# Dense rows as three exact bf16 parts times fp16 count panels, 16 panel groups, 336 edge tiles counted

## The reference, cut to what matters

```python
def _L0_gnn_ref(x, edge_index, weight, bias):
    summed = jax.ops.segment_sum(x[src], dst, num_segments=n)
    deg = jax.ops.segment_sum(jnp.ones_like(src, dtype=x.dtype), dst, num_segments=n)
    agg = summed / jnp.maximum(deg, 1.0)[:, None]
    out = jnp.concatenate([x, agg], axis=-1) @ weight
    out = out / jnp.linalg.norm(out, axis=-1, keepdims=True)
    return out + bias

def _forward(feats, ...):                       # layer 1
    h = feats * jax.lax.rsqrt(deg_out)[:, None]
    m = jax.ops.segment_sum(h[src], dst, num_segments=n) * jax.lax.rsqrt(deg_in)[:, None]
    x = m @ W_gc + b_gc + (feats @ W_res + b_res)
    y = x + _moe_ff(x, Wg, bg, w1, b1, w2, b2)
    ...                                         # batch norm over the nodes

x = _layernorm(x + _L0_gnn_ref(x, edge_index, ...), axis=-1)
x = _layernorm(x + _L1_gnn_ref(x, ..., src, dst), axis=-1)
```

## Time and profile before

| | |
|---|---|
| median of 3 runs | 2753.98 us (2734.45 to 2765.64) |
| the profiled execution | 2723.63 us, its span 2721.7 us |
| granted clock of TensorE, mean | 0.889 |
| PE busy | 2033.4 us, 75% |
| DVE, ACT, POOL busy | 1284.5, 605.1, 1364.6 us |
| moved by DMA | 304.32 MB |
| layer 0's steps | about 57 to 946 us of the span |
| layer 1's steps | about 1053 to 1888 us |

### The profile page before, as it was taken

One profiled execution on the slowest core, in us unless ns is written; L12 is line 12 of the kernel. 1 busy time (PEld: TensorE's weight loads), 2 busy tenths in 40 slices (PEclk: granted clock), 3 DMA queues, 4 the chain that ended last, 5 costly groups with the idle time before them and its releaser, 6 DMA issues.

```text
span 2721.7 us, 49652 instructions
## 1 busy us (share of the span) xinstructions
PE 2033.4 (75%) x15088; PEld 1633.2 (60%) x15088; DVE 1284.5 (47%) x3827; ACT 605.1 (22%) x1544; POOL 1364.6 (50%) x1353
## 2 busy tenths in 40 slices
PE   2788888888787573788888888885653788888847
PEld 1566666767666451567666666763542677777735
DVE  6655666766665484433433333322434232232275
ACT  0211112212121052211111211111323222222227
POOL 4655566556556674555555455564446334443410
PEclk9788899999998795899999999997776899999968
DMA  4323333333323504322232233234100776547772
GB/s 150 97 88 91 89 89 104 94 94 108 92 86 88 173 6 143 88 86 82 82 87 83 72 88 88 78 89 162 43 31 18 218 230 206 158 132 220 216 226 98
DMA packets 217122, 304.32 MB, mean 112 GB/s; under 512 B 46418, under 2 KB 164233, under 8 KB 216956
## 3 DMA queue, kind: packets, MB, share of 16 engines
q0 software_dynamic: 58576, 146.85, 18.8%
q1 hardware_dynamic: 103388, 101.82, 11.7%
q10 hardware_dynamic: 54992, 53.49, 6.2%
HBM read 289.58 MB, written 57.83 MB: 128 GB/s over the span
## 4 chain that ended last, share of the span: by engine, by line
PE 43%; issue 14%; DVE 14%; another core or an unknown queue 13%; SPq 6%; DMA 3%; DVEq 2%; ACT 2%; POOL 1%; POOLq 0%; ACTq 0%
PE bank L1095 16%; PE bank L1117 3%; PE bank L1051 3%; PE bank L1113 3%; PE bank L1131 3%; PE bank L1066 3%; PE bank L1294 3%; DVE oh_lo L1481 3%; PE bank L1303 2%; DVE oh_hi L1481 2%; PE bank L1192 2%; DVE Y L1898 1%; DVE codes L1503 1%; DMA acc<-x_scratch,acc 1%
## 5 line engine op out<-in xcount | busy, mean ns | idle before, releaser
L707 POOL DMA_INDIRECT gath<-in_x_dram,idx_t x480 | 532.7, 1110 | 393.8 <-PE bank L1051 242.7
L1095 PE MATMUL bank<-Y,X 128*128 128x128 f32 x5096 | 682.3, 289 | 28.2 <-issue 26.8
L1095 PEld LDWEIGHTS bank<-Y,X 128*128 128x128 f32 x5096 | 661.5, 204 | 58.6 <-issue 41.4
L707 POOL DMA_INDIRECT gath<-h_scratch,idx_t x480 | 467.6, 974 | 389.8 <-PE bank L1051 225.1
L837 ACT ACTIVATE Y<-bank 128x400 f32<-128x400 f32 (+1 forms) x416 | 184.1, 494 | 1066.0 <-remote 615.1
L1503 DVE TENSOR_SCALAR codes<-iota_code,code_t 128x784 bf16<-128x784 f16 x456 | 175.4, 426 | 274.2 <-remote 211.0
L1481 DVE TENSOR_TENSOR oh_lo<-iota_lo,lohi_t 128x512 bf16<-128x512 bf16 x392 | 269.2, 687 | 40.3 <-remote 32.0
L1515 DVE TENSOR_TENSOR acc<-acc,bank 128x256 f32 x240 | 101.2, 422 | 372.5 <-issue 356.1
L1113 PE MATMUL bank<-codes,oh_lo 128*128 128x400 bf16 x456 | 164.7, 362 | 121.1 <-DVE oh_hi L1481 54.8
L1117 PE MATMUL bank<-codes,oh_lo 128*128 128x384 bf16 x456 | 163.6, 359 | 79.0 <-issue 53.0
L802 POOL DMA_INDIRECT y_scratch<-acc x96 | 97.6, 1017 | 221.1 <-DVE acc L1875 206.2
(11 more groups left out here) (244 smaller groups left out, 2568.4 us busy)
## 6 DMA issues: line engine op xcount, KB each, us to landing
acc<-in_L_gnn_w_dram SPq DMA_DIRECT2D x101, 512.0 KB
acc<-in_L_gnn_w_dram ACTq DMA_DIRECT2D x96, 512.0 KB
y_scratch<-bias_s ACTq DMA_DIRECT2D x49, 256.0 KB
y_scratch<-bias_s SPq DMA_DIRECT2D x98, 128.0 KB
Y<-y_scratch SPq DMA_DIRECT2D x14, 896.0 KB
acc<-in_L_gnn_b_dram ACTq DMA_DIRECT2D x96, 128.0 KB
gath<-in_x_dram,idx_t POOLq DMA_INDIRECT x480
gath<-h_scratch,idx_t POOLq DMA_INDIRECT x480
```

Source lines behind the costliest of these rows:

```text
L707: pool.indirect_dma_start(out=gath[:, half, k, :], out_offset=None, in_=table, in_offset=bass.IndirectOffsetOnAxis(ap=idx_t[:, TD + t:TD + ...
L1095: last = pe.matmul(DB[w % 2][:, c * P:(c + 1) * P], X[:, h, c * P:(c + 1) * P], panel[:, w % 2, h, :], start=(h == 0), stop=(h == NT - 1))
```

## The change

Each fp32 number of X is split into three bf16 parts whose sum is the number: its upper 16 bits (`x_top`, read in place as every second bf16), the rest rounded to bf16 (`x_mid`, in Y's memory), and what is left (`x_low`, written over the lower 16 bits in X). The panels are kept in fp16, in half of Y, and a slice becomes three bf16 by fp16 products into the same bank. PE makes the rests (`rests`: identity in fp32 minus the top; `lows`: minus the middle) in the two banks of `dense`, which are free before the first group, and ACT copies them out; 25 cuts of two row tiles, six ahead of step 0 and four in each of the first five steps. As X no longer holds x after this, `turn_x` puts the three parts together by three products where the tile is cut already, and X is loaded again behind the last dense product, interleaved with Y. The plan grows from 304 to 336 counted tiles, with 8 more panels of two tiles and 16 of one; a layer has 56 steps, windows of three steps after a lead of two, 16 groups, and up to three panel additions a step. ACT clears `acc` in place of POOL.

```diff
-PANEL_TILES = ((8, 9), (4, 21), (2, 74))
-GROUP_PANELS = ((1, 1, 6),) * 9 + ((0, 2, 6), (0, 4, 4)) * 2
-WINDOW = 4
-ADDS = 2
+PANEL_TILES = ((8, 9), (4, 21), (2, 82), (1, 16))
+GROUP_PANELS = ((1, 1, 6, 0),) * 9 + ((0, 2, 6, 0), (0, 4, 4, 0)) * 2 + ((0, 0, 8, 0), (0, 0, 0, 8), (0, 0, 0, 8))
+WINDOW = 3
+LEAD = 2
+ADDS = 3
...
+    cut = [(i, 2) for i in range(NT - 2, 0, -2)] + [(0, 1)]
+    EARLY, PER_STEP = 6, 4
...
+    turned_whole = [cut_of[i] >= EARLY + PER_STEP * i + PER_STEP // 2 for i in range(NT)]
...
-            units_at[WINDOW * w + u * WINDOW // len(units)].append((w,) + unit)
+            units_at[WINDOW * w + LEAD + u * WINDOW // len(units)].append((w,) + unit)
         for k in range(WINDOW):
-            slices_at[WINDOW * (w + 1) + k] = (w, SLICES * k // WINDOW, SLICES * (k + 1) // WINDOW)
+            slices_at[WINDOW * (w + 1) + LEAD + k] = (w, SLICES * k // WINDOW, SLICES * (k + 1) // WINDOW)
...
-        panel = yflat.rearrange("p (b h n) -> p b h n", b=2, h=NT)
+        panel = yflat[:, 0:NT * P].bitcast(F16).rearrange("p (b h n) -> p b h n", b=2, h=NT)
+        x_mid = yflat[:, NT * P:2 * NT * P].bitcast(BF16).rearrange("p (t d) -> p t d", t=NT)
+        x_halves = X[:, :, :].rearrange("p t d -> p (t d)").bitcast(BF16).rearrange("p (t d k) -> p t d k", t=NT, k=2)
+        x_low, x_top = x_halves[:, :, :, 0], x_halves[:, :, :, 1]
+        x_parts = (x_top, x_mid, x_low)
...
                 for k in range(SEVEN):                      # SP, load_back
                     sp.dma_start(Y[:, SEVEN * k:SEVEN * (k + 1), :], ...).then_inc(y_back, 16)
+                    if L == 1:
+                        sp.dma_start(X[:, SEVEN * k:SEVEN * (k + 1), :], tile_rows(h_d, P * SEVEN * k, SEVEN, P)
+                                     ).then_inc(x_again, 16)
+                    ...                                     # the same from x in layer 0
...
-                    if L == 0 and t == 2 * GROUP:           # POOL
-                        pool.memset(acc[:, :, :], 0.0).then_inc(acc_step, 1)
...
+            pool.wait_ge(x_again, 16 * (SEVEN + 1))
             in_pairs(pool, NT, stage)
-            for b in range(2):
-                pool.wait_ge(sums_staged[b], (NT + 1 - b) // 2)
-            pool.memset(acc[:, :, :], 0.0).then_inc(acc_step, 1)
...
+            def keep_mids(L, first):                        # ACT; keep_lows alike: low_left, x_low, low_made
+                for k in range(first, min(first + 2, len(cut))):
+                    i, n = cut[k]
+                    act.wait_ge(rest_made, len(cut) * L + k + 1)
+                    act.activation(x_mid[:, i:i + n, :].rearrange("p t d -> p (t d)"), DB[k % 2][:, 0:n * D], ACT.Copy
+                                   ).then_inc(mid_made, 1)
...
             for st in range(ST):
+                first_cut = EARLY + PER_STEP * st
+                keep_mids(1, first_cut)
+                keep_lows(1, first_cut)
                 keep_panels(1, st)
                 if st < NT:
                     turned_x(1, st)
+                keep_mids(1, first_cut + 2)
                 keep_part(1, st)
+                keep_lows(1, first_cut + 2)
...
+            def rests(L, first):                            # PE
+                ...
+                    if k > 1:
+                        pe.wait_ge(low_made, q - 1)
+                    o = DB[k % 2][:, 0:n * D]
+                    pe.matmul(o, ident[:, :], X[:, i:i + n, :].rearrange("p t d -> p (t d)"), start=True, stop=False)
+                    pe.matmul(o, minus_i[:, :], x_top[:, i:i + n, :].rearrange("p t d -> p (t d)"),
+                              start=False, stop=True).then_inc(rest_made, 1)
+
+            def lows(L, first):
+                ...
+                    pe.wait_ge(mid_made, len(cut) * L + k + 1)
+                    pe.matmul(DB[k % 2][:, 0:n * D], minus_i[:, :], x_mid[:, i:i + n, :].rearrange("p t d -> p (t d)"),
+                              start=False, stop=True, skip_group_check=True).then_inc(low_left, 1)
...
-                    last = pe.matmul(DB[w % 2][:, c * P:(c + 1) * P], X[:, h, c * P:(c + 1) * P], panel[:, w % 2, h, :],
-                                     start=(h == 0), stop=(h == NT - 1))
+                    for k, part in enumerate(x_parts):
+                        last = pe.matmul(DB[w % 2][:, c * P:(c + 1) * P], part[:, h, c * P:(c + 1) * P], panel[:, w % 2, h, :],
+                                         start=(h == 0 and k == 0), stop=(h == NT - 1 and k == len(x_parts) - 1))
...
+                rests(L, first_cut)                         # in step, and again behind turn_x
                 dense(L, st, lo, lo + (hi - lo) // chunks)
                 if st > 0:
                     shift(L, st - 1)
+                lows(L, first_cut)                          # and again behind prep
```

More of the change, by code:

```diff
@@ L119, in gnn_kernel @@
     BY_DVE = 4
+    cut = [(i, 2) for i in range(NT - 2, 0, -2)] + [(0, 1)]
+    EARLY, PER_STEP = 6, 4
+    assert len(cut) <= EARLY + PER_STEP * (WINDOW + LEAD)
+    cut_of = {j: k for k, (i, n) in enumerate(cut) for j in range(i, i + n)}
+    turned_whole = [cut_of[i] >= EARLY + PER_STEP * i + PER_STEP // 2 for i in range(NT)]
     SLICES = DC * NT
@@ L847, in keep_part, with clear_sums @@
                                ACT.Copy).then_inc(part_ready, 1)
+            def clear_sums(cols):
+                n = cols.stop - cols.start if isinstance(cols, slice) else 2 * P
+                return act.activation(acc[:, :, cols], small[:, 12:13].unsqueeze(2).to_broadcast([P, DC, n]), ACT.Copy)
             act.wait_ge(fill_set, 2)
+            clear_sums(slice(0, ACCW)).then_inc(acc_step, 1)
+            for k in range(0, EARLY, 2):
+                keep_mids(0, k)
+                keep_lows(0, k)
             for st in range(ST):
+                first_cut = EARLY + PER_STEP * st
                 if st < NT:
@@ L1036, in _ @@
             pe.wait_ge(tabs_made, 4)
[L1037 removed]
+            pe.matmul(banks[1][0:1, 0:1], small[:, 9:10], ones_c[:, 0:1], start=True, stop=True
                       ).then_inc(flag_summed, 1)
+            pe.wait_ge(tabs_done, 2 * CH)
+            pe.wait_ge(const_set, 8)
+            groups_in = set()
+            def rests(L, first):
+                for k in range(first, min(first + 2, len(cut))):
+                    i, n = cut[k]
+                    q = len(cut) * L + k
+                    if L == 0:
+                        for g in sorted({i // SEVEN, (i + n - 1) // SEVEN} - groups_in):
+                            pe.wait_ge(x_in[g], 32 if g == SEVEN - 1 else 16)
+                            groups_in.add(g)
+                    if k > 1:
[5 more added lines that the diff above has]
+            def lows(L, first):
+                for k in range(first, min(first + 2, len(cut))):
+                    i, n = cut[k]
+                    pe.wait_ge(mid_made, len(cut) * L + k + 1)
+                    pe.matmul(DB[k % 2][:, 0:n * D], minus_i[:, :], x_mid[:, i:i + n, :].rearrange("p t d -> p (t d)"),
+                              start=False, stop=True, skip_group_check=True).then_inc(low_left, 1)
+            for k in range(0, min(EARLY, 8), 2):
+                rests(0, k)
+                lows(0, k)
             pe.wait_ge(win_set, 1)
[L1040 removed]
             pe.wait_ge(weights_in, 3 * 16)
+            for k in range(8, EARLY, 2):
+                rests(0, k)
+                lows(0, k)
             def sums(L, st):
@@ L1120, in turn_x @@
             def turn_x(L, i):
-                if L == 0 and i % SEVEN == 0:
-                    pe.wait_ge(x_in[i // SEVEN], 32 if i == NT - SEVEN else 16)
+                if L == 0 and i == 0:
+                    pe.wait_ge(x_in[0], 16)
                 wait_count(pe, prep_done, NT * L + i)
+                if not turned_whole[i]:
+                    pe.wait_ge(low_made, len(cut) * L + cut_of[i] + 1)
                 for c in range(DC):
-                    last = pe.transpose(TB[:, c * P:(c + 1) * P], X[:, i, c * P:(c + 1) * P], ident[:, :])
+                    if turned_whole[i]:
+                        last = pe.transpose(TB[:, c * P:(c + 1) * P], X[:, i, c * P:(c + 1) * P], ident[:, :])
+                        continue
+                    for k, part in enumerate(x_parts):
+                        last = pe.matmul(TB[:, c * P:(c + 1) * P], part[:, i, c * P:(c + 1) * P], minus_i[:, :],
+                                         start=(k == 0), stop=(k == len(x_parts) - 1))
                 last.then_inc(x_turned, 1)
@@ L1205, in _ @@
             pe.wait_ge(h_by_act, (SEVEN - BY_DVE) * NG7)
+            for k in range(0, EARLY, 2):
+                rests(1, k)
+                lows(1, k)
             for st in range(ST):
```

82 lines of the change are left out of this document (63 added, 19 removed).

## The result

The changed kernel took 3039.3 us (median of 4 runs, 3024.6 to 3053.9) beside 2744.2 for the kernel before: a ratio of 1.107, 95% interval [1.097, 1.118]. The forecast was 2767, the range ended at 2900.

The account below looks back on a forecast made before the run. PE, the busiest engine, was no plain bound; handshakes took the rest. Terms -14 - 44 + 32 + 25 + 14 = +13 us on the profiled 2723.6 gave 2737, forecast as 2767 for the median; range 2685 to 2900.

Parts of the forecast that it names:

- Records: Dense steps: PE pauses grow as records per step rise from 118 to about 172; +25 us, bounds 0 to +93.
- rival 2: Dense steps: PE pauses and late one-hots grow with records, ACT's cuts add 10; +91 us, median 2845, chance 0.22.
- handshakes: 48-step stretches of each layer: PE busy 83 and 82%, the rest taken as waiting between engines.
- steps with both kinds of work: Steps that build panels and run dense products, 45 in place of 48 a layer: -3 and -11, together -14 us.
- one multiply-only and one empty step fewer, two layers: Tail of each layer's steps: one multiply-only step and one with neither kind of work drop out; -44 us.
- start and cuts, two layers: Start of each layer: 25 cuts on PE, six ahead of step 0; +16 us a layer, +32 in all.
- between the layers (second load): After layer 0's dense products: DVE and POOL wait for Y and X being loaded again; +9 us of +14.
- behind layer 1's steps: After layer 1's dense products: the same wait for loading X again with Y; +5 us of +14.
- dense slice: Dense product: three bf16 products at 0.056 us make 0.168 a slice, so a step's dense work stays the same.
- rival 3: Dense product: strided top and low parts load slowly as weights; +260 us after slack, median about 3080, chance 0.13.
- Rival 1: Aggregation steps: gathers, sums and evacuation set a step's price, units cost evenly; -55 us, median 2699, chance 0.28.

Follow-up runs that it names:

- quiet: Occasions, kernels unaltered, where the kernel before takes 2232 to 2237 us (medians) and PE shows no pauses; changed kernel 2255.1, ratio 1.0094.
- paused: Occasions where the kernel before takes 2671 to 2754 us (medians) and PE stands still for no event the profile shows; changed kernel 3039.3, ratio 1.107.
- wide_parts: Changed kernel with dense operands changed over: panel stationary, 256 columns moving, half the dense products; 2268.5 and 2262.6 us quiet, 2744.9 paused (1.025).
- parts_alone: Three bf16 parts in the kernel before's panel groups (13 groups, four steps each); 2229.3 us quiet (0.997), 2921.5 paused (1.091).
- padded: Kernel before with two one-column bf16 products added behind each fp32 dense product; 2605.3 us quiet (1.165), 3320.8 paused (1.240).
- looped: Changed kernel with about 73% of the dense products in loops on PE; 2257.7 us quiet (1.012), 3002.9 paused (1.115).
- plain_gathers: Changed kernel with POOL's indirect gathers in the steps replaced by plain loads of 128 consecutive rows; 2240.5 us quiet, 2305.2 paused (0.861).

## Why the prediction was wrong

**The step that failed is "Records".** I had the mechanism as a rival (2: "the denser instruction stream feeds the pauses"); as a term of the sum I priced it at +25, at most +93. Its size was 276 us: 383 lost in the steps of the kernel before, 659 in the changed one. Three errors made that.
1. I counted idle time as the whole of the loss (130.6 + 127.6 us). But a pause is followed by products at half the clock, and that time is *busy*. The earlier trace rows had it in plain sight, 0.92 and 0.93 where quiet steps have 1.00; I called it "near the upper level". It is 73 us of the 190 in layer 0 (621.7 busy in the earlier trace rows, 548.3 quiet).
2. I let it grow by products, 118 to 172 a step (it became 176, and 90 to 146 in layer 1: 1.45 in all). The loss grew by 1.72. With the first two errors mended the term would have been 383 x 0.45 = 172 us; the other 104 are a loss per product that itself rose, for a reason that is open.
3. I took the value near the lower end because the largest waits name DVE's one-hots. But the 3.01 us wait of the earlier trace rows stands in a quiet step as well (2.98 us at 707.05 in the changed kernel), so that name doesn't tell paused from quiet.

Behind the third lies a misreading of the earlier trace rows, that PE's idle share of a step is handshakes: quiet, PE is busy for 97 and 100% of the steps of the kernel before.

The loss against the products, all the steps with both kinds of work (paused less quiet; products by the stretches' counts):

| | products a step, layers 0 / 1 | lost us a step | ns a product |
|---|---|---|---|
| kernel before | 118 / 90 | 3.95 / 4.0 | 33 / 45 |
| wide_parts | 127 / 97 | 4.1 / 3.9 | 32 / 40 |
| parts_alone | 146 / 119 | 6.3 / 5.7 | 43 / 48 |
| padded | 167 / 139 | 6.1 / 6.4 | 37 / 46 |
| changed kernel | 176 / 146 | 7.2 / 7.4 | 41 / 51 |
| looped | 176 / 146 | 5.9 / 7.3 | 33 / 50 |
| plain_gathers | 176 / 146 | 0.0 / 0.0 | 0 |

The rows come from three occasions, beside which the kernel before took 2744 (kernel before, changed kernel), 2682 (wide_parts, parts_alone, padded, plain_gathers) and 2696 us (looped). 62 us between occasions are up to 0.6 us a step, so small differences between rows say nothing.

More products go with more loss, 30 to 50 ns for each, while POOL issues indirect gathers. It isn't a fixed price of a product: a step of layer 1 has 23% fewer products than one of layer 0 in the kernel before and wide_parts, 17 to 19% fewer in the others, and loses about as much.

Shown: more products make the loss larger, their columns and the place of their code don't explain it, and with plain loads of consecutive rows it is gone. Not shown:
- Whether it goes by products or by weight loads. Each product here comes with a load of its own (PE and PEld have nearly the same counts in every row), the added one-column products too.
- Whether the form of the address matters or the rows that are read.
- By what path POOL's gathers hold up PE, and what makes an occasion paused. Nothing in a kernel of mine made the occasion come or go.
- Whether the recording itself takes part. The records of semaphore events get fewer exactly where PE pauses, and every time here comes with a clock and a span, that is, from an execution that was recorded. That rival was not tested.

**The other steps**, quiet and paused, changed less before, in us:

| term | forecast | quiet | paused |
|---|---|---|---|
| steps with both kinds of work | -14 | +1.6 | +277 |
| one multiply-only and one empty step fewer, two layers | -44 | -35 | -13 |
| start and cuts, two layers | +32 | +39 | +58 |
| between the layers (second load) | about +9 | +10 | +14 |
| behind layer 1's steps | about +5 | -8 | -5 |
| records, pauses | +25 | 0 | in the others |

The quiet column adds up to +7 (2239.7 to 2246.7), the paused one to +330. Where nothing pauses, every other term came out within 16 us, and 1.009 is the forecast of no change. That is luck in part: its prices of a step were read from paused rows (16.6 and 15.3 us a step forecast, 12.6 and 11.1 quiet), and errors of 16, 9 and 7 us one way, and of 13 and 25 the other, nearly cancel. The dense slice is 0.168 us: three starts in 0.17 above. That settles rival 3: the strided parts load as fast as the middle one. By the Trainium skill, "TensorE: Matmul & The Clock Gate", Back-to-back issue gap, it would be about 81 ns a product; the rows show 56 at the upper clock and 107 at the lower, so the measurement decides for 56. (The 3080 of rival 3 doesn't follow from its own terms either: 2767 + 260 = 3027.) The point from which rival 2 was to decide, idle of more than 4 us a step, was passed: 219.1/45 = 4.9 in layer 0, 4.2 in layer 1.

The second load: quiet, PE's first combinations wait 5.08 us for POOL's staging, which waits for X, where the kernel before has 17.01 us of products in a row.

```profile
763.83 2.05 PE L1312 MATMUL bank<-w_s,gath 128*128 128x256 f32 x4 [5.43 <-ACT gath L928]
770.96 6.26 PE L1312 MATMUL bank<-w_s,gath 128*128 128x256 f32 x20 [5.08 <-POOL gath L767]
```

Rival 1 (steps are what costs) fell too, even quiet: a step has no price of its own. Quiet, PE is busy for 95 to 100% of it, so PE's products set it.

## What to carry to other kernels

Before pricing a change to an engine, ask of the profile whether its waits with no event and its granted clock are the kernel's own or the occasion's: run the kernel again, and if the time is another, price the change in both conditions. A rewrite that trades few slow products for many fast ones of the same total time is neutral only while nothing holds up the issue of each. Where something does, count instructions: the form with half as many dense products (panel stationary, 256 columns moving) lost 2.5% where the other lost 10.7% on another paused occasion, and costs 0.6% when it is quiet. Put time at a lower clock beside idle time when a stall is added up.

## What the runs showed that I had not expected

- The kernel before ran at 2232 to 2237 and at 2671 to 2754 us (medians), some 20% apart, while executions of one kernel beside each other agree to about 1.5%.
- Four pauses of 0.35 to 1.01 us were followed by products at 0.107 us from start to start, half the clock; the low clock costs seven tenths of what the idle time does (134.7 against 190.8 us in layer 0).
- Two one-column bf16 products behind each fp32 product cost 0.126 us together, more than the two of 128 columns that a slice of the changed kernel has besides its first (0.112); most of it shows before them, not in them.
- 256 moving columns of a part take as long as two products of 128: the 45 steps of layer 1 are 500.7 us with 98 dense products a step and 501.9 with 49.
- In paused stretches the trace holds under half of the semaphore events of quiet ones (3965 against 8781), in both kernels.
